# Attention that stores undivided sums channel by channel, and a row projection that divides and reads them with a step of four

## The chip, the cores and the metric

The kernel runs on one core of a Trainium2 chip. A core has a matrix engine (TensorE, PE in the profile, with its weight loads listed apart as PEld), VectorE (DVE), ScalarE (ACT), GpSimd (POOL) and a queue processor (SyncE, SP). Transfers between the chip's memory (DRAM here) and the core's SBUF are moved by 16 DMA engines. The metric is the device time of one launch in microseconds, as the median of some runs; lower is better.

## What is computed

One transformer layer on x of shape (4, 2048, 256), all in float32. Cut to what matters here:

```
y    = softmax(causal(q k^T / 4)) v          16 heads of 16 channels, per batch of 2048 tokens
x1   = x + concat_heads(y) @ Wc              the row projection: 8192 tokens x 256 channels
n    = layernorm(x1);  logits = n @ Wr + br  the router, 8 experts, top 2
out  = x1 + sum over 2 experts of gate * (relu(n @ W1 + b1) @ W2 + b2)
```

The change is in how y is divided by its softmax sums and how it reaches `y @ Wc`.

## The kernel before

The kernel is written as four stages, one behind another with a barrier between each: `project` (layernorm and the products that make q, k and v), `attend`, `mix` (the row projection, second layernorm and router) and `experts`. Each engine runs a list of instructions in its order and waits on semaphores.

**attend** goes through 16 windows w. A window is one batch and a group of GH = 4 heads over all 2048 tokens. It has CH = 4 chunks of TB = 512 query tokens, and chunk c has 4(c+1) steps of 128 key tokens, so a window has NSTEP = 40 steps. Three kinds of work are interleaved on TensorE. A `max` piece (L1004) makes scores of 128 queries of two heads in a bank pair `ps_m`, and VectorE takes their maxima (L888, and L892 on the diagonal); this runs a window ahead. A `scores` group (L963) makes transposed scores with the maximum already taken off, and ScalarE takes their exponential (L865). A `sum` step (L984) multiplies four heads' exponentials by v with a column of ones, into `ps_o`: per head, 16 rows of values and a 17th that is the softmax sum, 32 partitions apart, with the 512 queries along the row. After a chunk's last step ScalarE copies `ps_o` to `out_sb` (L871).

A fourth kind, `turn_out`, stands 64 times in the list (16 windows, 4 chunks). TensorE turns the chunk's `out_sb` with four transposes into a `ps_m` slot (L1015), VectorE takes the reciprocal of the sums (L926) and multiplies (L931) into `y_sb`, and SP stores 128 KB to `y_dram`, in which a row is a token (L757).

What sets the order of the four kinds is `attention_plan`, run when the kernel is built: it keeps estimated clocks of the engines and picks the kind that can start first, shifted by `HOLD`. All engines walk the same list, `PLAN`. The `ps_m` slots are two, used in turn (`ring`), and TensorE waits for a slot's last reader before it writes it.

On SP's queue, behind the last step of window w, stand 13 transfers that load window w+3 (L716 and L724, 256 KB each but the last), then the store of the last chunk, then the maxima of the next window (L733 and L739), and so on, as `PLAN` has them.

**mix** goes through NB = 16 tiles of 512 tokens in NB+2 iterations. TensorE turns the loaded rows of y (`turn_y`, L1452), ScalarE copies them to `yt` (L1206), TensorE multiplies by Wc (`mix_heads`, L1467), VectorE adds x to make `x1` (L1328) and takes the layernorm. ScalarE applies it, TensorE turns the result, forms the logits (L1479), and two iterations later VectorE picks the two experts and makes `slots`, whereon GpSimd issues 8 indirect transfers for the tile that scatter entries to `list_dram` (L1189, 128 in all). SP loads y and x four tiles ahead (`load_y` L1136, `load_x` L1139), stores x1 (L1161) and fetches a part of the expert weights per tile (L1143). A tile's token t = 4q + j is partition q, row j.

**experts** begins with loads of `list_dram`, so it waits for all 128 scatters, and walks 142 tiles of 128 rows.

## Time and profile before

| | us |
|---|---|
| median of 3 runs | 2670.48 |
| lowest and highest | 2664.89, 2671.22 |
| the profiled execution, its own time | 2660.48 |
| its span, first to last instruction | 2658.8 |
| granted TensorE clock, mean of the span | 0.948 |

Busy time in the span: TensorE 2356.7 us (89%), VectorE 2044.3 (77%), ScalarE 1581.8 (59%), GpSimd 824.5 (31%). The stages stand in the trace roughly so: `project` to about 260 us, `attend` to 1930, `mix` to 2131, `experts` to the end. A busy time is an average over stages with different limits, so the stages have to be read apart.

### The profile page before, as it was taken

The page shows a single profiled execution, that of the slowest core. Times are in us where ns is not written, and L with a number is a line of the kernel's source. Part 1 is how long each engine was busy: PE and PEld are TensorE (multiplying, and loading weights), DVE is VectorE, ACT ScalarE, POOL GpSimd, SP SyncE. Part 2 cuts the span into 40 slices and gives each one's busy share as a digit, 9 for nine tenths or more (in the row PEclk, how much of TensorE's full clock was granted, in tenths as well). Part 3 has the DMA queues.
Part 4 walks back from the last instruction along what each step waited for, and adds up shares of the span by engine and source line. Part 5 has one row for each costly group of instructions (what it writes and reads, how often), then busy time and mean ns, then how long its engine had stood idle before and what let it go on. Part 6 is the DMA issues. An engine that isn't in the chain of part 4 may idle for free. (4 is left out here: it accounts for less than half of the span.)

```text
span 2658.8 us, 48214 instructions
## 1 busy us (share of the span) xinstructions
PE 2356.7 (89%) x15842; PEld 1342.6 (50%) x15842; DVE 2044.3 (77%) x5000; ACT 1581.8 (59%) x2716; POOL 824.5 (31%) x1132
## 2 busy tenths in 40 slices
PE   6786699999999999999999999998879379999998
PEld 6675233333343333333333333333256168998897
DVE  3785988988989899888889988993068557777776
ACT  3663177776777777766777777777745234444443
POOL 1444021121122112112112112112137755566554
PEclk7998599999999999999999999999989689999999
DMA  3777824135045045044144144101099323333332
GB/s 136 260 267 222 118 45 76 41 60 119 30 63 89 28 65 89 28 64 76 42 63 74 45 65 73 45 8 31 21 296 281 115 89 114 107 105 109 111 110 71
DMA packets 147718, 256.02 MB, mean 96 GB/s; under 512 B 72968, under 2 KB 92042, under 8 KB 139157
## 3 DMA queue, kind: packets, MB, share of 16 engines
q1 hardware_dynamic: 114544, 164.96, 28.0%
q0 software_dynamic: 29904, 80.65, 9.2%
q10 hardware_dynamic: 3028, 7.33, 1.7%
q8 instruction: 135, 2.21, 0.4%
q14 instruction: 107, 0.87, 0.1%
HBM read 147.65 MB, written 107.76 MB: 96 GB/s over the span
## 5 line engine op out<-in xcount | busy, mean ns | idle before, releaser
L865 ACT ACTIVATE prob<-ps_s 128x512 f32<-128x512 f32 (+5 forms) x1620 | 1078.5, 714 | 464.8 <-PE ps_s L963 462.2
L888 DVE TENSOR_REDUCE maxes<-ps_m 128x2 f32<-128x1024 f32 x768 | 914.1, 1222 | 112.6 <-PE ps_m L1004 109.3
L963 PE MATMUL ps_s<-q_st,k_st 50*128 50x512 f32 (+3 forms) x2560 | 605.4, 409 | 78.9 <-ACT prob L865 56.9
L1004 PE MATMUL ps_m<-k_st,q_st 48*128 48x512 f32 (+3 forms) x2560 | 605.1, 444 | 75.2 <-DVE maxes L888 39.6
L814 POOL TENSOR_SCALAR_AFFINE_SELECT prob<-prob 128x256 f32<-128x256 f32 x512 | 203.2, 406 | 1341.8 <-ACT prob L865 1211.9
L984 PE MATMUL ps_o<-prob,v_sb 128*17 128x512 f32 (+3 forms) x5120 | 606.7, 547 | 1.4 <-ACT prob L865 0.7
L1004 PEld LDWEIGHTS ps_m<-k_st,q_st 48*128 48x128 f32 x2560 | 273.6, 192 | 531.2 <-DVE maxes L888 261.3
L892 DVE CUSTOM_DVE_ANT_0 junk<-ps_m,causal 128x128 f32<-128x128 f32 (+3 forms) x1024 | 453.0, 484 | 47.6 <-PE ps_m L1004 45.9
L963 PEld LDWEIGHTS ps_s<-q_st,k_st 50*128 50x128 f32 x2560 | 316.6, 188 | 299.9 <-ACT prob L865 222.0
L1741 ACT ACTIVATE h_hi<-ps_turned 128x512 fp32r<-128x512 f32 x142 | 84.9, 598 | 213.9 <-PE ps_turned L1856 212.4
L94 PE MATMUL ps_out<-experts_hi,h_lo 128*128 (+1 forms) x568 | 171.6, 302 | 0.1
L984 PEld LDWEIGHTS ps_o<-prob,v_sb 128*17 128x17 f32 x5120 | 86.5, 95 | 168.5 <-issue 138.4
L96 PE MATMUL ps_out<-experts_hi,h_hi 128*128 (+1 forms) x568 | 160.4, 282 | 0.0
L95 PE MATMUL ps_out<-experts_lo,h_hi 128*128 (+1 forms) x568 | 160.1, 282 | 0.0
L1189 POOL DMA_INDIRECT list_dram<-entry,slots x128 | 123.9, 968 | 76.2 <-issue 39.6
L1770 DVE TENSOR_TENSOR h<-ps_hidden,b_sb 128x512 f32<-128x512 f32 x142 | 98.3, 692 | 43.9 <-PE ps_hidden L96 43.4
L1784 DVE TENSOR_TENSOR y<-ps_out,b_sb 128x256 f32<-128x256 f32 x142 | 60.3, 425 | 87.0 <-PE ps_out L96 87.0
L94 PE MATMUL ps_hidden<-experts_hi,x_lo 128*128 (+1 forms) x284 | 125.5, 442 | 0.3 <-issue 0.2
L96 PE MATMUL ps_hidden<-experts_hi,x_hi 128*128 (+1 forms) x284 | 112.6, 396 | 0.0
L95 PE MATMUL ps_hidden<-experts_lo,x_hi 128*128 (+1 forms) x284 | 112.4, 396 | 0.0
L1731 ACT ACTIVATE xn<-rows,lists 128x256 f32<-128x256 f32 x142 | 84.0, 591 | 47.1 <-DMA rows<-rows_dram,lists 46.2
L95 PEld LDWEIGHTS ps_out<-experts_lo,h_hi 128*128 128x128 f32 x568 | 107.6, 189 | 0.1
(187 smaller groups left out, 3065.8 us busy)
## 6 DMA issues: line engine op xcount, KB each, us to landing
parts_dram<-parts SPq DMA_DIRECT2D x64, 512.0 KB, 3.8
q_st<-parts_dram SPq DMA_DIRECT2D x84, 256.0 KB, 8.9
k_st<-parts_dram SPq DMA_DIRECT2D x84, 256.0 KB, 18.2
v_dram<-v_out SPq DMA_DIRECT2D x16, 544.0 KB, 5.5
xin<-in_L_attn_x SPq DMA_DIRECT2D x16, 512.0 KB, 6.0
ffn_raw<-in_L_ffn_W POOLq DMA_DIRECT2D x32, 256.0 KB, 5.2
y_dram<-y_sb SPq DMA_DIRECT2D x64, 128.0 KB, 2.0
split_hi<-ffn_hi POOLq DMA_DIRECT2D x16, 512.0 KB, 3.2
```

The source lines that it names most:

```text
L94: nc.tensor.matmul(out, s_lo, m_hi, start=first, stop=False, skip_group_check=True)
L95: nc.tensor.matmul(out, s_hi, m_lo, start=False, stop=False, skip_group_check=True)
L96: return nc.tensor.matmul(out, s_hi, m_hi, start=False, stop=last, skip_group_check=True)
L814: nc.gpsimd.affine_select(out=tile, in_=tile, compare_op=ALU.is_ge, fill=0.0, base=0, pattern=[[0, 2], [1, P]], channel_multiplier=-1).the ...
L865: last_exp = nc.scalar.activation(prob[:, at:at + n, lo:TB], bank[:, 0:n, lo:TB], ACT.Exp, scale=DH ** -0.5)
L888: return nc.vector.tensor_reduce(maxes[:, 2 * pair:2 * pair + 2, qt, kc], bank[:, :, :], AX.X, ALU.max)
L892: last = nc.vector.tensor_tensor_reduce(junk[:, slot, i, 0:w], bank[:, i, 0:w], causal[:, TB - w:TB], 1.0, NEG, ALU.add, ALU.max, maxes[:, ...
L963: mm = nc.tensor.matmul(ps_s[k % 2][:, i, lo:TB], k_st[half(h % 2, ROWS), w % BUFS, h // 2, kt * P:(kt + 1) * P], q_st[half(h % 2, ROWS), ...
L984: mm = nc.tensor.matmul(ps_o[32 * h:32 * h + VW, lo:TB], v_sb[:, w % BUFS, kt, h, :], prob[:, (s % PROBS) * GH + h, lo:TB], start=STEP_FIR ...
L1004: mm = nc.tensor.matmul(ps_m[slot][:, i, 0:wide], q_st[half(i, STACK), w % BUFS, pair, qt * P:(qt + 1) * P], k_st[half(i, STACK), w % BUFS ...
L1189: pool.indirect_dma_start(list_dram[:, :], bass.IndirectOffsetOnAxis(ap=slots[:, j, i:i + 1], axis=0), entry[:, j, i, :], None).then_inc(s ...
L1770: nc.vector.tensor_tensor(out=h[:, s % 2, :], in0=ps_h[s % 2][:, :], in1=b1_sb[:, bass.ds(e, 1), :].rearrange("p a n -> p (a n)"), op=ALU. ...
```

## The change

**In attend**, `turn_out` is gone: the four transposes, the reciprocal and the product of a chunk, with `y_sb` and `rec`. SP stores `out_sb` as it is, 256 KB a chunk, to a `y_dram` whose row is a channel (32 rows for each of the 16 heads: 16 of values, the sum, the rest unused) and whose columns are the 8192 tokens. Sums are divided apart: at step 3 of window w, SP loads the 2048 x 4 sums of window w-1 as 128 rows of 64; at step 12 VectorE takes their reciprocal in place; at step 20 SP stores them to `inverse_dram`, one row per head. ScalarE's copy of chunks 0 and 1 waits for the stores of the window before. `PLAN` is made anew without `turn_out`, so pieces shift against each other. A helper transfer of numbers (L834) is replaced by an iota on GpSimd.

**In mix**, `turn_y` and ScalarE's copy to `yt` are gone. A tile of y is loaded as two transfers of 8 heads x 16 channels x 512 tokens, and the inverses as two more of the same size, each head's row repeated for its 16 channels. VectorE multiplies the two in place (`scale_heads`, 128 x 1024). The product with Wc takes its stationary operand from the scaled tile directly; since token t = 4q + j must come to partition q, 128 columns are read with a step of four elements. The last window's sums are fetched, inverted and stored at the start of mix.

```diff
-                elif e[0] == "turn_out":
-                    ...
-                    sp.dma_start(to.rearrange("(j p) n -> p j n", p=P),
-                                 y_sb[:, c % 2, :, :, :].rearrange("p j h d -> p j (h d)")
-                                 ).then_inc(y_stored[c % 2], 16)
+                elif e[0] == "sum":
+                    w, c, _ = STEP_LIST[e[1]]
+                    step = e[1] % NSTEP
+                    if w and step == INVERSE_LOAD:
+                        for u in range(2):
+                            sp.wait_ge(y_stored[u], 32 * w)
+                        ...
+                        load_sums(sp, w - 1, inverse[:, (w - 1) % 2, :], sums_in)
+                    elif w and step == INVERSE_STORE:
+                        sp.wait_ge(inverse_made, w)
+                        store_inverse(...)
+                    if STEP_LAST[e[1]]:
+                        sp.wait_ge(out_copied, w * CH + c + 1)
+                        sp.dma_start(y_dram[w % HG * P:(w % HG + 1) * P, ...], out_sb[:, c, :])
+                    if e[1] + 1 == (w + 1) * NSTEP and w + BUFS < NG:
+                        sp.wait_ge(summed, e[1] + 1)
+                        load(sp, w + BUFS)
...
+                elif e[0] == "sum" and e[1] >= NSTEP and e[1] % NSTEP == INVERSE_MADE:
+                    w = e[1] // NSTEP - 1
+                    dve.wait_ge(sums_in, 16 * (w + 1))
+                    nc.vector.reciprocal(inverse[:, w % 2, :], inverse[:, w % 2, :]).then_inc(inverse_made, 1)
...
+                for a in range(CC):
+                    sp.dma_start(y_in[:, n % YB, a, :],
+                                 y_v[a * HP:(a + 1) * HP, 0:DH, tokens]).then_inc(y_loaded[n % YB], 16)
...
+                    sp.dma_start(inverse_in[:, n % 2, a, :],
+                                 inverse_dram[a * HP:(a + 1) * HP, tokens].unsqueeze(1).broadcast_to([HP, DH, TB])
+                                 ).then_inc(y_loaded[n % YB], 16)
...
+                if n + 2 < NB:
+                    sp.wait_ge(y_scaled, n + 1)
+                    load_inverse(n + 2)
...
+            def scale_heads(n):
+                dve.wait_ge(y_loaded[n % YB], 32 * CC * (n // YB + 1))
+                tt(out=y_in[:, n % YB, :, :], in0=y_in[:, n % YB, :, :], in1=inverse_in[:, n % 2, :, :],
+                   op=ALU.mult).then_inc(y_scaled, 1)
...
-                                                yt[:, a, j * P:(j + 1) * P], wc_sb[:, a, :],
+                                                y_in[:, n % YB, a, :].rearrange("p (q j) -> p j q", j=TILES)[:, j, :], wc_sb[:, a, :],
```

TensorE in attend, from the last step of chunk 0 to the first of chunk 1 of window 6 (`ps_m` maxima, `ps_s` scores, `ps_o` sums; a row is a line, an output, its inputs and its shape). Before:

```order
L984 MATMUL ps_o<-prob,v_sb 17x128 x4
L1004 MATMUL ps_m<-k_st,q_st 128x256 x2
L963 MATMUL ps_s<-q_st,k_st 128x384 x2
L1004 MATMUL ps_m<-k_st,q_st 128x256 x2
L963 MATMUL ps_s<-q_st,k_st 128x384
L1015 MATMUL ps_m<-ident,out_sb 128x128 x4
L984 MATMUL ps_o<-prob,v_sb 17x512 x4
```

and in the changed kernel, whose lines have other numbers (L988 is the sum, L1008 the maxima, L967 the scores):

```order
L988 MATMUL ps_o<-prob,v_sb 17x128 x4
L967 MATMUL ps_s<-q_st,k_st 128x384 x2
L1008 MATMUL ps_m<-k_st,q_st 128x512 x2
L967 MATMUL ps_s<-q_st,k_st 128x384
L1008 MATMUL ps_m<-k_st,q_st 128x256 x2
L988 MATMUL ps_o<-prob,v_sb 17x512 x4
```

The four transposes are gone, and the maxima stand in other places beside the same scores.

SP in attend, around the load of a window (q, k and v to `q_st`, `k_st`, `v_sb`). Before:

```order
L716 DMA q_st<-parts_dram 16x2x2048 x6
L716 DMA k_st<-parts_dram 16x2x2048 x6
L724 DMA v_sb<-v_dram 128x1088
L757 DMA y_dram<-y_sb 128x4x64
L733 DMA minus_dram<-minus_rows 16x2x128
L739 DMA q_st<-minus_dram 2x2x512 x2
```

and in the changed kernel:

```order
L769 DMA y_dram<-out_sb 128x512
L708 DMA q_st<-parts_dram 16x2x2048 x6
L708 DMA k_st<-parts_dram 16x2x2048 x6
L716 DMA v_sb<-v_dram 128x1088
L721 DMA inverse<-y_dram 128x1x64
L769 DMA y_dram<-out_sb 128x512
L734 DMA minus_dram<-minus_rows 16x2x128
L740 DMA q_st<-minus_dram 2x2x512 x2
```

The last chunk's store has moved ahead of the 13 loads, and the sums are fetched directly behind them.

SP in mix, one tile. Before (x rows, expert weights, then y of the tile four ahead; `b_sb` and `x_own` are the buffers of y and x):

```order
L1161 DMA rows_dram<-x 128x1024
L1139 DMA x_own<-in_L_attn_x 128x1024
L1143 DMA experts_lo<-split_lo 128x2048
L1136 DMA b_sb<-y_dram 128x1024
```

and in the changed kernel:

```order
L1171 DMA rows_dram<-x 128x1024
L1144 DMA x_own<-in_L_attn_x 128x1024
L1148 DMA experts_lo<-split_lo 128x2048
L1131 DMA b_sb<-y_dram 128x1x512 x2
L1139 DMA inverse_in<-inverse_dram 128x1x512 x2
```

The y load is two transfers in place of one, of the same bytes, and two of inverses, again the same bytes, stand behind it.

## Rows read from the trace of the kernel before

**Rows 1.** Busy time by stretch: us, then busy (instructions) per engine, PEclk, DMA share, GB/s.

```profile
430.00:1834.00 1404.00, 1302.82 (x9224) 541.45 (x9224) 1235.51 (x2689) 1016.37 (x1618) 262.38 (x532) 0.98 0.33 59
1834.00:1930.00 96.00, 78.03 (x501) 26.01 (x497) 3.41 (x10) 72.06 (x118) 17.12 (x36) 0.98 0.06 19
1970.00:2060.00 90.00, 82.30 (x552) 59.31 (x551) 74.52 (x482) 50.35 (x102) 68.35 (x72) 1.00 1.01 274
```

**Rows 2.** Groups by line: busy us, mean ns of one, idle before it and its releaser.

```profile
L1015 PE MATMUL ps_m<-ident,out_sb 128*128 128x128 f32 x256 | 42.2, 288 | 9.3 <-DVE maxes L888 4.9 <-DVE maxes L892 1.5 <-ACT out_sb L871 1.4
L931 DVE TENSOR_TENSOR y_sb<-ps_m,rec 128x256 f32<-128x256 f32 x64 | 27.2, 424 | 4.7 <-DMA y_dram<-y_sb 2.6
L926 DVE RECIPROCAL rec<-ps_m 128x16 f32<-128x16 f32 x64 | 16.2, 254 | 112.0 <-PE ps_m L1015 111.1
L888 DVE TENSOR_REDUCE maxes<-ps_m 128x2 f32<-128x1024 f32 x768 | 914.1, 1222 | 112.6 <-PE ps_m L1004 109.3
L386 DVE TENSOR_TENSOR turned<-turned,swapped 128x512 f32<-128x512 f32 x32 | 21.5, 711 | 0.0
```

**Rows 3.** The tile y_sb: who waited for it (us, times).

```profile
  PE ps_m L1004: 3.3, 4
```

**Rows 4.** Timeline, the end of attend: start, us, engine, line.

```profile
1925.79 0.58 ACT L871 COPY out_sb<-ps_o 128x512 f32<-128x512 f32 x1 [1.17 <-PE ps_o L984]
...
1927.92 0.36 SPq L757 DMA_DIRECT2D y_dram<-y_sb  x1
1930.35 0.36 ACTq L1199 DMA_DIRECT2D numbers<-in_tile_numbers  x1
```

**Rows 5.** Timeline of SP at a window's end, the load of the next.

```profile
1030.54 2.66 SPq L716 DMA_DIRECT2D q_st<-parts_dram  x6
...
1036.04 0.42 SPq L724 DMA_DIRECT2D v_sb<-v_dram  x1
1036.50 0.44 SPq L757 DMA_DIRECT2D y_dram<-y_sb  x1
```

**Rows 6.** Tile y_sb in 1030 to 1045 us: landing of that store.

```profile
DMA to landing us min/median/max: 22.8/22.8/22.8
```

**Rows 7.** Timeline of ACT: copy of that window's last chunk, next window's chunk 1.

```profile
1030.61 0.59 ACT L871 COPY out_sb<-ps_o 128x512 f32<-128x512 f32 x1
...
1058.74 0.59 ACT L871 COPY out_sb<-ps_o 128x512 f32<-128x512 f32 x1
```

**Rows 8.** Stretches as in rows 1: mix before scatters; head loads; two small transfers.

```profile
1950.00:1960.00 10.00, 8.45 (x47) 5.91 (x46) 7.53 (x32) 6.34 (x13) 0.00 (x0) 1.00 1.00 385
...
1038.00:1054.00 16.00, 15.07 (x123) 6.97 (x125) 15.48 (x43) 11.66 (x21) 3.15 (x8) 1.00 1.03 126
...
512.60:513.60 1.00, 0.38 (x5) 0.02 (x2) 1.00 (x2) 1.00 (x2) 0.00 (x0) 1.00 0.09 37
```

**Rows 9.** DMA issues in 509 to 514 us: KB each.

```profile
q_st<-minus_dram SPq DMA_DIRECT2D x2, 24.0 KB
```

**Rows 10.** DMA issues in 1970 to 2060 us: KB each, median us to landing.

```profile
rows_dram<-x SPq DMA_DIRECT2D x10, 512.0 KB, 12.5
experts_hi<-split_hi SPq DMA_DIRECT2D x5, 1024.0 KB
...
b_sb<-y_dram SPq DMA_DIRECT2D x7, 512.0 KB, 17.5
```

**Rows 11.** Timeline of mix: the same step of two tiles on DVE.

```profile
2009.74 1.29 DVE L1328 TENSOR_TENSOR x<-ps_x,x_own 128x512 f32<-128x512 f32 x2
...
2018.52 1.29 DVE L1328 TENSOR_TENSOR x<-ps_x,x_own 128x512 f32<-128x512 f32 x2
```

**Rows 12.** Line 1467, the product with Wc: duration ns min/median/max.

```profile
L1467 PEld LDWEIGHTS ps_x<-wc_sb,yt x256: 186/190/337, 1938.5 to 2068.3; 128*128 128x128 f32 x128
L1467 PE MATMUL ps_x<-wc_sb,yt x256: 379/379/792, 1938.5 to 2068.5; 128*128 128x256 f32 x128
```

**Rows 13.** Timeline of POOL: first scatters of mix, last scatter.

```profile
1966.69 1.05 POOL L1189 DMA_INDIRECT list_dram<-entry,slots  x1 [34.80 <-DVE slots L1437]
...
1984.61 0.96 POOL L1189 DMA_INDIRECT list_dram<-entry,slots  x1 [0.30 <-issue]
...
2130.96 0.97 POOL L1189 DMA_INDIRECT list_dram<-entry,slots  x1 [0.31 <-issue]
```

More of the change, by code:

```diff
@@ L473 @@
 BUFS = 3
-HOLD = {"max": -171, "scores": -140, "sum": 0, "turn_out": -266}
+HOLD = {"max": -171, "scores": -140, "sum": 0}
+HEAD_ROWS = 32
+INVERSE_LOAD, INVERSE_MADE, INVERSE_STORE = 3, 12, 20
 STEP_LIST = [(w, c, kt) for w in range(NG) for c in range(CH)
@@ L593, in attention_plan @@
             k += 1
-        elif kind == "sum":
+        else:
             plan.append(("sum", s))
@@ L603, in attention_plan, with attend @@
                 loaded[s // NSTEP + BUFS - 1] = end + 45000
-        else:
-            plan.append(("turn_out", outs.pop(0)[0]))
-            tile_free[:], issued = [start + 430, start + 430], start + 430
-            vector = max(start + 630, vector - 85) + 700
-            taken.append(vector)
     return plan
-def attend(nc, parts_dram, v_dram, w1, w2, minus_dram, y_dram, split_dram, tile_numbers, rows_dram, pairs_dram,
+def attend(nc, inverse_done, parts_dram, v_dram, w1, w2, minus_dram, y_dram, inverse_dram, split_dram, rows_dram, pairs_dram,
            list_dram):
@@ L1029, with mix @@
 XB = 4
-def mix(nc, x, y_dram, wc, wr, br, split_dram, tile_numbers, w_sb, b1, b2, biases, biases_in, block, slots_made, scattered, numbers, run, entry, slots, rows_dram,
+def mix(nc, inverse_done, x, y_dram, inverse_dram, wc, wr, br, split_dram, tile_numbers, w_sb, b1, b2, biases, biases_in, block, slots_made, scattered, numbers, run, entry, slots, rows_dram,
         pairs_dram, list_dram):
@@ new lines, in transformer_block @@
+    with ExitStack() as whole:
+        inverse_done = [whole.enter_context(nc.semaphore(name))
+                        for name in ("sums_in", "inverse_made", "inverse_stored0", "inverse_stored1")]
+        attend(nc, inverse_done, parts_dram, v_dram, w["L0_ffn_W1"], w["L0_ffn_W2"], minus_dram, y_dram, inverse_dram, split_dram,
+               rows_dram, pairs_dram, list_dram)
+        with ExitStack() as ctx:
+            w_sb = [ctx.enter_context(nc.sbuf_tensor(f"experts_{half}", [P, CHUNKS, WCH], F32R)) for half in ("hi", "lo")]
+            biases = [ctx.enter_context(nc.sbuf_tensor(name, [P, E, width], F32))
+                      for name, width in (("b1_sb", F), ("b2_sb", C))]
+            biases_in = ctx.enter_context(nc.semaphore("biases_in"))
+            slots_made = ctx.enter_context(nc.semaphore("slots_made"))
+            scattered = ctx.enter_context(nc.semaphore("scattered"))
+            block = ctx.enter_context(nc.Block())
+            numbers = ctx.enter_context(nc.sbuf_tensor("numbers", [P, SLOT_TILES], F32))
+            run = ctx.enter_context(nc.sbuf_tensor("run", [P, 2, TOP, E], F32))
+            entry = ctx.enter_context(nc.sbuf_tensor("entry", [P, NT, TOP, WORDS], I32))
+            slots = ctx.enter_context(nc.sbuf_tensor("slots", [P, NT, TOP], I32))
+            mix(nc, inverse_done, w["L0_attn_x"], y_dram, inverse_dram, w["L0_attn_Wc"], w["L0_ffn_Wr"], w["L0_ffn_br"], split_dram,
+                w["tile_numbers"], w_sb, w["L0_ffn_b1"], w["L0_ffn_b2"], biases, biases_in, block, slots_made, scattered, numbers, run, entry, slots, rows_dram, pairs_dram, list_dram)
+            experts(nc, block, slots_made, scattered, w_sb, numbers, run[:, NB % 2, :, :], entry, slots, biases, biases_in, rows_dram, pairs_dram,
+                    list_dram, out)
```

155 lines of the change are left out of this document (62 added, 93 removed).

## The prediction

> **What bounds the kernel now.** I read the stretches of the busy-time table first, then the groups by line, then the timeline where an edit lies. In `attend` (first line of [rows 1]) PE is busy for 1302.8 of 1404 us and DVE for 1235.5; a `turn_out` is work for both, and each waits for the other on the two `ps_m` slots. Taking work from both shortens the stage, and neither can hide the other's saving. In the last window (second line of [rows 1]) ACT has 72 of 96 us and DVE 3: little is won there. In `mix` (third line of [rows 1]) the DMA engines are full (share 1.01, 274 GB/s), and one thing stands behind them: GpSimd's scatters. The first starts at 1966.69, the last at 2130.96 [rows 13]; 127 steps in 164.3 us are 1.29 us each, so a tile's eight take 10.2 to 10.3, nearly without a pause. `experts` waits for all of them. So `mix` ends when POOL ends, and POOL is fed by DVE, which is fed by loads. A DVE tile takes 8.78 us [rows 11], the DMA's pace, and runs ahead of POOL. Whatever makes a tile's loads longer than 10.2 us moves the end.
>
> **Attend, what goes.** PE: 64 groups of transposes are 42.2 us busy, 9.3 idle ahead of them [rows 2], and 3.3 in which the next maxima waited for `y_sb` [rows 3]: 54.8. Windows 0 to 14 hold 60 of the 64: 51. DVE: 16.2 (reciprocals) + 27.2 (products) + 2.6 (wait for a store) = 46.0 [rows 2], by 60/64: 43. Both are full, so the gain lies between; DVE's maxima wait for PE for 109.3 us in all [rows 2], which are PE's rhythm, not free time. I take 45, bounds 43 to 51; only if the freed slots are not filled (the remaining pieces follow other dependencies) does it fall to half. The end: the last copy starts at 1925.79 and ends at 1926.37, transposes, product and a store at 1927.92 follow, and `mix` begins at 1930.35 [rows 4]. The store now follows the copy: about -2.
>
> **Attend, what comes.** One reciprocal a window, 128x64, 15 times. The 128x16 one takes 254 ns (L926 in [rows 2]), and 64 elements at the maxima's 1222 / 1024 ns (L888) are 76: 0.2 to 0.33 us each, +3. Its wait is the new thing: DVE stands at step 12 until the sums are in, and all maxima queue behind it. The sums' transfer stands directly behind the 13 loads, 3.7 MB, which began at 1030.54 [rows 5] and run at 126 GB/s with the queue full (second line of [rows 8]). The store that stood there, issued at 1036.50, landed 22.8 us later [rows 5, 6], at 1059.3, which is 28.7 us after the window's copy at 1030.61; chunk 1 of the next window was copied at 1058.74 [rows 7], 28.1 us in, and step 12 is the end of that chunk's steps. So the sums come at about 29 to 32 and DVE asks at about 31 to 33. I take +3 for 13 windows; bounds 0 and, if each stands 2 to 4 us, 26 to 52. Ahead of the loads SP now also waits for the last chunk's copy, 0.6 us [rows 7], inside that. ACT's new wait, for a store from a window before, is for transfers that stand ahead of the loads and have a chunk's time to land: 0. The inverses' store at step 20 has 80 us to land: 0. Dropping `first_numbers` is 0 (one load, once).
> Sum of attend: -45 - 2 + 3 + 3 = **-41**.
>
> **Mix, engines.** PE loses a tile's transposes, ACT a copy: neither sets the pace (POOL and the DMA do): 0. DVE gains a product of 128x1024 from SBUF. The 128x512 one on SBUF takes 0.71 (L386 in [rows 2]), twice that 1.42; a reduction of 1024 takes 1.22. DVE's share of a stretch is 74.5 of 90 [rows 1], 7.3 us a tile; 8.7 fits below 10.2: 0, while it would cost 16 x 1.4 = 22 if DVE were the bound. The operand read with a step of four: weight loads of 190 ns between products of 379 [rows 12], 16 a tile; nothing shows what a step costs. Bounds: nothing, or loads three times as long, 16 x 0.38 = 6.1 us a tile. PE is busy for 82.3 of 90 us [rows 1], 8.0 of a tile; 8.0 + 6.1 = 14.1, less the transposes that it loses, which is still about the DMA's tile below. So 0, but under rival 1 it would cost from 2 us a tile on.
> The Trainium skill, page "SBUF — State Buffer", section "Door 1: The DMA port swizzle", has SBUF lines of 16 bytes, and each access that goes to a new line pays; a step of four float32 is a new line for each element. No row of before shows such a read. By that the weight loads would be longer; the sum would not change as long as they stay covered.
>
> **Mix, transfers.** The two loads of y are the same bytes, and 0.5 MB of inverses is added to a tile of y 0.5, x 0.5, rows 0.5, experts 1.0 MB [rows 10]. What decides is how many engines carry the new forms. Two transfers whose outer count is 2 (24 KB in all) [rows 9] were under way in 512.6 to 513.6 and the share there was 0.09 at 37 GB/s (third line of [rows 8]): 0.09 x 16 = 1.5, so about two engines out of 16. The new loads have an outer count of 8 (heads), against 128 before. I take 8 of the 16 engines, the same ones each time.
> The Trainium skill, page "DMA: Bandwidth & Descriptors", section "Why a DMA increments its semaphore by 16 and not by 1", says just this: the number of engines is the largest up to 16 that divides the slowest dimension of both sides, here 8 and 128, the lowest-numbered ones. The row of the two agrees.
> Speed of an engine: 385 GB/s at share 1.00 before the scatters (first line of [rows 8]), 24.1 each. Under scatters it is 274 [rows 1]: 24.6 MB in 90 us would take 64 at 385; the 26 lost fall on 90 / 1.27 = 71 scatters, 0.38 us each. On a low engine a tile is now y 65.5 KB + inverses 65.5 + a sixteenth of 2.0 MB, 131: 262 KB / 24.1 = 10.9 us, + 8 x 0.38 = **13.9 us**, over POOL's 10.2.
> The last tile's inverses have ahead of them on such an engine 3.90 MB (y and inverses of 16 tiles 2.10, x 0.52, rows and experts of 13 tiles 1.28): 162 us, + 11 tiles of scatters 33, + 4 to start: from 1930 to 2129. In that iteration `slots` of tile 11 follows, at 2131.5, and from there POOL has tiles 11 to 15, 40 scatters at 1.27, 51 us: 2182 against 2132. **+50.** Bounds: if all 16 engines carried them, a tile would be 3.0 MB / 385 = 7.8 + 3.0 = 10.8 us, +0.6 on POOL's 10.2 for a dozen tiles: +8; if the pieces of 2 KB went at the head loads' 126 / 16 = 7.9 GB/s an engine, each tile of y would take 8.3 rather than 2.7 us, 5.6 x 16 = 90 more: +140. I take +50, since mix's own loads are nearer in kind.
>
> **Sum.** 2660.5 - 41 + 50 = 2669.5 on the profiled execution's time. The median of three is 10.0 above that one: **2679**, +0.3%.
>
> **The rivals.**
> (1) Other side, faster: the 16 engines share the loads, or scatters don't slow an engine that is already the late one. Then mix is POOL's, the row stage costs +8 and not +50, the rest is -33: 2638. It decides by whether a tile on the loads' engines stays under 10.2 us. For it: without the 3.0 a tile has 10.9; against it: the row of the two-part transfers.
> (2) The small pieces are slow: +90 on the forecast: 2769. For it: 126 GB/s under the head loads; against it: those are other strides, and y is read in long rows.
> (3) The sums come late and DVE stands 2 to 4 us in each of 13 windows, 26 to 52 in place of 3: 2702 to 2728. For it: the landing at 28.7 is within 3 us of when it is asked for, and one window's rhythm is not another's. Against: DVE is itself late in a window.
> (4) Attend gains only half, -20 in place of -41: 2700. The plan's estimates are not of the chip, and pieces moved; PE may turn out to wait for ACT. ACT has 72% of its time [rows 1], so it is not next by much, but its exponentials follow the scores.
> (5) That the change doesn't do what it says: the order of instructions shows the transposes gone and the loads in place, so no chance of its own.
>
> **How the numbers follow.** Forecast 0.45, with its own range from 2663 to 2695 (attend by 43 to 51, the scatters' part of 3.0 a tile by a third either way). Rival 1 0.25, rival 2 0.07, rival 3 0.10, rival 4 0.13. The range: 2632 (rival 1 with an attend of -47) to 2712 (rival 4, half of rival 3); rival 2 and the rest of 3 are outside. About 8 us, 0.3%, is what a measurement of this kernel can tell from no change. Below 2662: rival 1 and a little of the forecast, 0.26. Within 2662 to 2678: some 0.20 of the forecast and 0.02 of others, 0.22. Above: 0.52.
>
> **What would show it.** Attend: its windows some 2.6 us shorter (41 / 16), no wait of DVE on `y_dram` data before the reciprocal above 1 us (rival 3 if 2 to 4). Mix: DVE's tile period near 13.9 with its wait on a load of `inverse_in`, DMA share about 0.8 (half of the engines at 13.9 of 13.9 us, the others at 5.4 + 3.0), POOL idle between tiles for DVE's `slots`, last scatter near 2141. Rival 1: period 10.2 to 10.8, share near 1.0, POOL unbroken. Rival 2: period near 20. Weight loads of L1467's successor longer than 190 ns but PE waited for by nobody. It is wrong above all if the new loads use more engines than 8, and if DVE's wait for sums is long.

## The result, and the profile after

The changed kernel takes 2740.44 us (median of four, 2727.90 to 2756.70), the kernel before 2670.85 beside it: a ratio of 1.0266 with a 95% interval of 1.0209 to 1.0324. Ratios, here and below, are taken over fast executions alone and can differ a little from the quotient of the two medians. The forecast was 2679 in a range up to 2712; the time lies 28 us above the range, and the change is slower by 70 us.

The stages, from the last copy of `out_sb` and the last scatter in each trace:

| | before | after |
|---|---|---|
| start to the last copy of attend | 1925.8 | 1935.9 |
| from there to the last scatter (row stage) | 205.2 | 273.2 |
| `experts` | 527.7 | 527.5 |

So 10 us are lost up to the end of attend, where 41 were to be won, and 68 in the row stage, where 50 were to be lost. (The 10 us are this pair's: over all traces, below, attend is as long as before.) Stretches of the changed kernel (us, then busy and instructions per engine, PEclk, DMA share, GB/s), to be held against [rows 1]:

```profile
430.00:1834.00 1404.00, 1297.87 (x8960) 525.67 (x8958) 1200.68 (x2585) 1013.05 (x1610) 260.97 (x527) 0.95 0.33 65
1936.00:2209.00 273.00, 148.12 (x738) 104.82 (x738) 149.90 (x838) 63.51 (x129) 126.04 (x133) 0.76 0.68 200
2000.00:2100.00 100.00, 64.56 (x330) 45.71 (x328) 58.10 (x329) 28.55 (x59) 53.49 (x55) 0.83 0.78 225
```

In attend TensorE is as busy as before, with the transposes gone, but its clock is 0.95 of full and not 0.98: it needs longer for the same products. In the row stage every engine idles (TensorE is busy for 148 of 273 us, GpSimd for 126), and the DMA share is 0.78 with 225 GB/s, where it was 1.01 with 274. It would look so if some of the 16 engines were full and others not; the experiments test it.

Who waits in the row stage (engine and line, what for, us, times, longest):

```profile
POOL list_dram L1199 <- DVE slots L1460: 106.2, 14, 63.9
DVE rank L1261 <- DMA numbers<-in_tile_numbers: 100.9, 1, 100.9
DVE b_sb L1332 <- DMA inverse_in<-inverse_dram: 85.1, 14, 10.1
```

GpSimd, without a pause in the kernel before [rows 13], waits 106 us for `slots`, 63.9 of them ahead of its first scatter (34.8 before). VectorE, which makes them, waits 85 us for the inverses, in 14 of 16 tiles (the second row is its idle time through the last window of attend). Three scatters with their waits, and the last two loads that gate:

```profile
2004.57 1.07 POOL L1199 DMA_INDIRECT list_dram<-entry,slots  x1 [63.94 <-DVE slots L1460]
...
2120.85 0.97 POOL L1199 DMA_INDIRECT list_dram<-entry,slots  x1 [5.81 <-DVE slots L1460]
...
2134.81 0.97 POOL L1199 DMA_INDIRECT list_dram<-entry,slots  x1 [4.08 <-DVE slots L1460]
```

```profile
2117.99 1.23 DVE L1332 TENSOR_TENSOR b_sb<-b_sb,inverse_in 128x1024 f32<-128x1024 f32 x1 [7.20 <-DMA inverse_in<-inverse_dram]
2119.90 0.17 DVE L1460 CAST slots<-slot 128x8 int32<-128x8 f32 x1
2131.95 1.22 DVE L1332 TENSOR_TENSOR b_sb<-b_sb,inverse_in 128x1024 f32<-128x1024 f32 x1 [5.46 <-DMA inverse_in<-inverse_dram]
2133.86 0.17 DVE L1460 CAST slots<-slot 128x8 int32<-128x8 f32 x1
```

The first scatter comes 68.7 us after the last copy (40.9 before), since the slots of tile 0 stand on VectorE behind the scaling of tile 4, and so behind five tiles of loads. From tile 0 to tile 9 a tile takes 14.5 us ((2134.81 - 2004.57) / 9) and each has a wait. From tile 9 on GpSimd is the bound, as it was all along before. So of the 68 us some 28 are the later first scatter and some 38 the nine tiles, 14.5 us each against 10.2.

The new instructions themselves:

```profile
L1332 DVE TENSOR_TENSOR b_sb<-b_sb,inverse_in 128x1024 f32<-128x1024 f32 x16 | 19.6, 1224 | 85.1 <-DMA inverse_in<-inverse_dram 85.1
L937 DVE RECIPROCAL inverse<-inverse 128x64 f32<-128x64 f32 x15 | 8.2, 548 | 51.3 <-DMA inverse<-y_dram 51.3
```

```profile
L1486 PEld LDWEIGHTS ps_x<-wc_sb,b_sb x256: 307/329/337, 1959.5 to 2158.4; 128*128 128x128 f32 x128
L1486 PE MATMUL ps_x<-wc_sb,b_sb x256: 379/420/812, 1959.5 to 2158.6; 128*128 128x256 f32 x128
```

Against [rows 12] a weight load with a step of four takes 329 ns in place of 190.

### The profile page after: what moved, and what is told of

It is laid out like the page before. It is cut to its first block and busy times, and to the rows that moved or that the text cites. A ratio compares the mean times of both kernels' runs of the same rounds, so it can differ in the third digit from the quotient of the medians.

```text
span 2736.6 us, 47289 instructions
## 1 busy us (share of the span) xinstructions
PE 2368.8 (87%) x15458; PEld 1335.0 (49%) x15458; DVE 2027.9 (74%) x4904; ACT 1566.0 (57%) x2684; POOL 828.1 (30%) x1132
## 5 line engine op out<-in xcount | busy, mean ns | idle before, releaser
L967 PE MATMUL ps_s<-q_st,k_st 50*128 50x512 f32 (+3 forms) x2560 | 619.9, 415 | 79.0 <-ACT prob L874 52.6
L1008 PE MATMUL ps_m<-k_st,q_st 48*128 48x512 f32 (+3 forms) x2560 | 607.1, 450 | 90.1 <-DVE maxes L900 49.4
L988 PE MATMUL ps_o<-prob,v_sb 128*17 128x512 f32 (+3 forms) x5120 | 628.7, 564 | 1.8 <-ACT prob L874 0.7
L1008 PEld LDWEIGHTS ps_m<-k_st,q_st 48*128 48x128 f32 x2560 | 273.5, 194 | 587.3 <-DVE maxes L900 300.7
L967 PEld LDWEIGHTS ps_s<-q_st,k_st 50*128 50x128 f32 x2560 | 324.4, 193 | 306.3 <-ACT prob L874 226.3
L988 PEld LDWEIGHTS ps_o<-prob,v_sb 128*17 128x17 f32 x5120 | 86.8, 96 | 176.1 <-issue 141.9
L1486 PE MATMUL ps_x<-wc_sb,b_sb 128*128 128x256 f32 x256 | 87.0, 512 | 70.2 <-DVE x L1349 52.0
L1486 PEld LDWEIGHTS ps_x<-wc_sb,b_sb 128*128 128x128 f32 x256 | 72.6, 329 | 81.6 <-issue 41.2
```

Source lines behind the costliest of these rows:

```text
L967: mm = nc.tensor.matmul(ps_s[k % 2][:, i, lo:TB], k_st[half(h % 2, ROWS), w % BUFS, h // 2, kt * P:(kt + 1) * P], q_st[half(h % 2, ROWS), ...
L988: mm = nc.tensor.matmul(ps_o[32 * h:32 * h + VW, lo:TB], v_sb[:, w % BUFS, kt, h, :], prob[:, (s % PROBS) * GH + h, lo:TB], start=STEP_FIR ...
L1008: mm = nc.tensor.matmul(ps_m[slot][:, i, 0:wide], q_st[half(i, STACK), w % BUFS, pair, qt * P:(qt + 1) * P], k_st[half(i, STACK), w % BUFS ...
L1486: last = nc.tensor.matmul(ps_x[j // 2][:, (j % 2) * C:(j % 2 + 1) * C], y_in[:, n % YB, a, :].rearrange("p (q j) -> p j q", j=TILES)[:, j, ...
```

## The experiments

They ran on five chips, and the chips are of two kinds. On two, as on the first, the kernel before takes 2672 to 2676 us; on three, 2730 to 2743. So each run is read against the runs of the kernel before on its own chip, and stage times are compared within a kind.

### Two kinds of chip

The kernel before was profiled three times more. In `before_b`:

> The kernel before, profiled on the chip of the runs beside it. On the chip of the last four runs it took 2730 us where it takes 2670 on the first, and the changed kernel 2769 where it takes 2740. If that chip is only slower in all stages alike, the row stage and the experts are here as long as there (205 and 528 us) times one factor. If signals arrive late in the row stage and the experts, as the traces of the four runs show (TensorE done, the next engine starting 2 to 6 us after it), the extra stands in those two stages alone and attend is 1499 us again, with 40 to 80 us at half clock.

It took 2680.11 us, with a row stage of 205.5 and `experts` of 527.7, on a chip of the first kind; its attend had 123 us at half clock, where 40 to 80 were expected. `before_c`:

> The kernel before once more, for its clock: its two traces show 59 and 125 us at half clock in attend with a length of 1499 and 1522 us from the fourth chunk's copy to the last, the changed attend 118 to 183 us in six traces. If the clock is the same lottery in both, this one lies anywhere between 59 and 183; if the changed order loses more, it is under 130. The length less 0.37 times the half-clock time is 1475 to 1478 in either case.

2735.01 us, row stage 246.7, `experts` 553.0, on a chip of the second. And `before_d`, of the second kind too:

> The kernel before, a fourth trace: half-clock time in attend under 130 us (so far 59, 125, 75), its length less 0.37 times that 1475 to 1480. Over 130 us would say that the changed attend's 116 to 181 are the same lottery.

2732.16 us, 245.6 and 548.5. On the second kind attend is no longer (1506 and 1509 us from the fourth copy to the last, 1499 and 1522 on the first), and the row stage and `experts` lose 41 and 21 to 25 us: so it is not one factor on all stages. What the traces show in these two stages, on all three chips of the second kind and on none of the first, are late signals. Waits of the row stage in `before_c`, and the tile that shows one:

```profile
ACT xt L1206 <- remote: 39.5, 9, 6.8
```

```profile
2061.17 1.04 PE L1452 MATMUL ps_turn<-ident,xn 128*128 128x128 f32 x8
...
2065.98 1.08 ACT L1206 COPY xt<-ps_turn 128x512 f32<-128x512 f32 x2 [5.59 <-remote]
```

TensorE ends its transposes at 2062.21, ScalarE starts on them 3.8 us later, and nothing of the kernel lies between ("remote": no releaser in the profile). On such a chip the kernel before itself no longer keeps GpSimd fed, so the change costs less there. What delays the signals stays open, and so does whether they are all of the 60 us.

### The changed kernel again

> The changed kernel beside it on the same chip: 2728 to 2770 us. Attend (first chunk copies to the last) 5 to 20 us longer than in the kernel before, with 130 to 185 us at half clock against some 60; row stage 68 to 80 us longer.

On the chip of `before_b`: 2728.25 us, ratio 1.0196 (1.0159 to 1.0233), row stage 272.4, 67 us over `before_b`. Attend is 10 us shorter than in `before_b` (1511 against 1522) and not 5 to 20 longer, because `before_b` itself lost much clock.

> The changed kernel beside the others on this chip: ratio to the kernel before 1.015 to 1.03, 116 to 181 us at half clock in attend.

On another of the first kind: 2735.58 us, ratio 1.0251 (1.0194 to 1.0308), row stage 269.2, 126 us at half clock: as expected.

> The changed kernel as it is, beside the others on one chip. In its first trace the row stage was 273 us (last copy of attend at 1935.9, last scatter at 2209.1) and attend had 163 us at half clock, against 59 in the kernel before. Both theories: 2728 to 2757 us. If the clock's loss belongs to the changed order of TensorE's work, half-clock time in attend is again over 110 us; if it was chance, it lies anywhere between 40 and 170.

On one of the second kind: 2769.20 us against 2729.56, ratio 1.0169 (1.0110 to 1.0228), row stage 286.9. That is 12 us over the expected time, which was worked out for a chip of the first kind; the half-clock time, 130 us, is over 110 as expected for an effect of the changed order.

### Row stage: the eight engines

The loads with an outer count of 16:

```diff
-                                 y_v[a * HP:(a + 1) * HP, 0:DH, tokens]).then_inc(...)
+                                 y_v[a * HP:(a + 1) * HP, 0:DH, tokens].rearrange("h d n -> d h n")).then_inc(...)
...
-                                 inverse_dram[a * HP:(a + 1) * HP, tokens].unsqueeze(1).broadcast_to([HP, DH, TB])
+                                 inverse_dram[a * HP:(a + 1) * HP, tokens].unsqueeze(0).broadcast_to([DH, HP, TB])
```

> The loads of y and of the inverses, and Wc, take channels in the order (channel of the head, head), so that the outer count of each load is 16 and no longer 8; nothing else is changed. If eight engines carrying the new loads set the pace of the row stage: a tile falls from 14 to 10.8 us or less, DMA share rises from 0.77 to near 1, and the time falls by 35 to 50 us. If the stage is paced by the longer weight loads (329 ns with the step of four) and its late start: less than 10 us.

2755.02 us, ratio 1.0100 (1.0062 to 1.0138) beside 1.0169 of the changed kernel on the same chip: 14 us by the medians. Row stage 259.7 against 286.9, less by 27. DMA share:

```profile
2000.00:2100.00 100.00, 64.72 (x322) 43.69 (x322) 60.40 (x333) 28.21 (x57) 60.54 (x59) 0.85 0.95 235
```

0.95 with 235 GB/s, where `after_again` has 0.75 with 224 in this stretch on the same chip: with nothing else changed than the order of channels, the same bytes keep more of the engines busy. Each busy engine moves less (15.5 GB/s against 18.7), so the share alone does not measure the gain. The gain is 14 to 27 us and not 35 to 50, and 19 of the 27 are the earlier first scatter (52.4 us after the last copy against 71.3). On this chip a tile can hardly get shorter: it still takes 13.5 us, with `slots` held up by late signals, as in `before_c` (13.4).

The inverses' loads left out:

```diff
+                if n >= 2:
+                    return
                 tokens = slice(n * TB, (n + 1) * TB)
                 for a in range(CC):
                     sp.dma_start(inverse_in[:, n % 2, a, :],
```

> The loads of the inverses are left out from the third tile on (the inverses of the first two tiles are used again, so y is divided by other tokens' sums); y is still loaded over an outer count of 8. A low engine's tile loses 65.5 KB of 262, 2.7 us by 24.1 GB/s: from 13.9 to 11.2 us. If the bytes on eight engines set the pace, the row stage falls by some 30 to 40 us. If the step of four or the late start does, by less than 10.

2687.64 us, ratio 1.0063 (1.0042 to 1.0085) beside 1.0196 on the same chip: 41 us by the medians. Row stage 222.5 against 272.4, less by 50, somewhat more than expected. 16 of the 50 are the earlier first scatter (53.8 us after the last copy against 69.7), 34 the shorter tiles: 10.5 us each up to tile 9. GpSimd hardly waits behind its first scatter (51.6 us in all, 49.1 of them ahead of it). So the bytes of the inverses are the pace, and the step of four, which is still in it, is not; that it matters over how many engines bytes lie is what `spread` shows. One rival is left: the inverses are asked for two tiles ahead and y four. In `after` those of tile 13 were asked for at 2112.73 and scaled at 2131.95, 19 us later; no run asked for them earlier, so how much of VectorE's wait is the short lead is not known.

Both the outer count of 16 and weights without a step:

```diff
-                tt(out=y_in[:, n % YB, :, :], in0=y_in[:, n % YB, :, :], in1=inverse_in[:, n % 2, :, :],
-                   op=ALU.mult).then_inc(y_scaled, 1)
+                tt(out=yt[:, n % 2, :, :].rearrange("p a (j q) -> p a j q", j=TILES),
+                   in0=y_in[:, n % YB, :, :].rearrange("p a (q j) -> p a j q", j=TILES),
+                   in1=inverse_in[:, n % 2, :, :].rearrange("p a (q j) -> p a j q", j=TILES),
+                   op=ALU.mult).then_inc(y_scaled, 1)
```

> Loads of y and inverses with an outer count of 16, as in the run spread, and the scaled y written by VectorE in the order that TensorE reads, so that the weight loads have no step. If the eight engines are what costs, most of the gain is that of spread (20 to 30 us of the changed kernel's row stage of 273) and the weights add under 5. If TensorE's chain (weights of 329 ns against 190, 2.2 us a tile) is next in line once the loads are spread, both together give 40 to 60 us.

In the trace the row stage is 238.3, 34 less, with the DMA share at 1.01. The times say less: 2716.93 us, ratio 1.0175 (1.0151 to 1.0200) beside 1.0196, and the intervals overlap; the profiled execution, 2692.42, was the fastest of five. VectorE pays for the reordering:

```profile
L1337 DVE TENSOR_TENSOR yt<-b_sb,inverse_in 128x1024 f32<-128x1024 f32 x16 | 32.0, 1999 | 36.8 <-DMA inverse_in<-inverse_dram 36.7
```

1999 ns where the plain product takes 1224. How much of the 34 us is the weights' and how much the engines' is not known: `spread` and this run stand on chips of different kinds.

The late start:

```diff
+            sp.dma_start(wr_sb[:, :, :], wr.rearrange("(a p) n -> p a n", p=P)).then_inc(weights_in, 16)
+            sp.dma_start(br_sb[:, :], br.rearrange("(e a) -> e a", a=1)).then_inc(weights_in, 16)
             load_y(0)
```

> The router's weights and bias are asked for ahead of everything else in the row stage; in the changed kernel TensorE waited for them until 1959.5, behind the loads of two tiles, with its first tile scaled at 1951.6. If the late start is paid once and never made up: 8 to 20 us less. If the eight loaded engines set the end, they have the same bytes to carry and the start changes nothing: 0 to 4 us.

2775.41 us, ratio 1.0149 (1.0102 to 1.0196) beside 1.0169; row stage 288.7 against 286.9. TensorE's 8 us wait for the router's weights is real and costs nothing: the loads behind set the end.

### Row stage: no bytes added

```diff
+            def expand(n, a):
+                ...
+                nc.tensor.matmul(ps_i[:, :], spread[:, :], inverse_in[0:HP, n % 2, a, :], start=True, stop=True
+                                 ).then_inc(expanded, 1)
...
-                tt(out=y_in[:, n % YB, :, :], in0=y_in[:, n % YB, :, :], in1=inverse_in[:, n % 2, :, :],
+                tt(out=y_in[:, n % YB, a, :], in0=y_in[:, n % YB, a, :], in1=ps_i[:, :],
```

> The changed kernel with the inverses loaded once per head (8 rows of 2 x 512) and spread to the 16 channels by TensorE, one product with a matrix of zeros and ones per half tile into a bank of its own, from which VectorE multiplies (two of 128x512, the second behind the slots); channels in the order (channel, head), so that y is read over an outer count of 16; the router's weights are asked for first. A tile moves 2.5 MB as in the kernel before. If bytes and their eight engines are the whole of the row stage's loss: the row stage falls from 272 to 205 to 215 us (GpSimd's scatters without pause), the run 50 to 65 us under the changed kernel and 0 to 15 us around the kernel before. If the step of four or TensorE's chain sets the pace: still over 230.

2767.76 us, ratio 1.0108 (1.0050 to 1.0165), on a chip of the second kind; its row stage of 276.7 is 10 us shorter than the changed kernel's on another such chip, and 30 longer than that of the kernel before on its own. The expectation missed. A likely reason, not tested by itself, is that each tile has two more hand-overs between TensorE and VectorE, and on this kind of chip hand-overs are what is slow. On a chip of the first kind the same row stage took 234.9 (in `all_three`, below), and not 205 to 215. Of the 30 us over the kernel before, 21 are the later first scatter (61.9 us after the last copy against 40.9), and a tile takes 11.0 us up to tile 9 against 10.2; TensorE is now near its limit, 91 of 100 us busy.

```profile
2020.00:2120.00 100.00, 91.40 (x471) 58.23 (x470) 77.10 (x433) 36.24 (x74) 70.60 (x73) 0.97 0.91 237
```

### Attend: the transposes and the clock

The old order of attend is back, with its transposes, and nothing uses them:

```diff
+                elif e[0] == "turn_out":
+                    dve.wait_ge(piece_made, ring + 1)
+                    nc.vector.tensor_copy(seen[:, e[1], :], ps_m[slot][:, 0, 0:4]).then_inc(piece_taken, 1)
...
+                        for j in range(TILES):
+                            mm = nc.tensor.transpose(ps_m[slot][:, 0, j * P:(j + 1) * P],
+                                                     out_sb[:, e[1] % CH, j * P:(j + 1) * P], ident[:, :])
```

> The changed kernel with the old order of attend: the four transposes of each chunk stand where they stood, VectorE only reads 4 columns of them (64 times some 0.1 us), and nothing uses the result. TensorE has its 42 us of transposes again. If their absence is what lets the clock fall: half-clock time in attend falls from 163 us to under 80, and the stage is no longer than with them gone, the whole run -15 to +5 against the changed kernel. If the clock is chance or has another cause: half-clock time as in the changed kernel, and the run 20 to 45 us longer than it.

2792.81 us, ratio 1.0220 (1.0176 to 1.0264), 24 us over the changed kernel on its chip; half-clock time in attend 160 us. By this one trace the transposes' absence is not what lets the clock fall. With these traces a simple law came out. Half-clock time is the time at 1.2 GHz in the trace's record of the granted clock; the length is from the fourth copy of `out_sb` to the last:

| | length, us | half clock, us | length - 0.37 x half clock |
|---|---|---|---|
| before | 1499.2 | 58 | 1477.7 |
| before_b | 1521.7 | 123 | 1476.2 |
| before_c | 1506.1 | 75 | 1478.3 |
| before_d | 1509.4 | 85 | 1477.8 |
| turns_kept | 1538.2 | 160 | 1478.8 |
| after | 1514.3 | 164 | 1453.7 |
| after_again | 1504.7 | 130 | 1456.7 |
| after_b | 1511.4 | 157 | 1453.3 |
| after_c | 1501.1 | 126 | 1454.3 |
| spread, early, no_inverse, spread_packed, expand (attend unchanged) | 1497.5 to 1523.7 | 116 to 181 | 1454.0 to 1456.8 |
| sums_later | 1494.6 | 119 | 1450.4 |
| expand_sums | 1517.1 | 178 | 1451.4 |
| maxima_later | 1523.1 | 208 | 1446.2 |
| all_three | 1529.8 | 228 | 1445.4 |
| tail_filled (55 products more) | 1522.5 | 171 | 1459.4 |
| expand_tail (55 products more) | 1559.0 | 276 | 1456.8 |

The factor is a line through the nine traces of the changed attend (0.365; the four of the kernel before give 0.342). Both kinds of chip lie on it. So, at equal clock (the last column), the changed attend is 23 us shorter, and with the old order and its transposes back and VectorE's part of `turn_out` all but gone (64 reads of 4 columns) it is as long as before. The 23 us are the transposes' and those of their place in the order; which of the two is not told apart. VectorE's 43 were worth at most the few us that the new wait for the sums costs in `turns_kept` too (4.4 us in one window). And in the mean the changed attend has 152 us at half clock in place of 85, which takes 0.37 x 67 = 25 us back: its mean length is 1510.7 us, and 1509.1 before. Most of the difference stands behind the last maxima: 37 to 96 us at half clock there in the nine traces (mean 67), 3 to 14 in the four of the kernel before (mean 6). In `after` this is the stretch, where the kernel before has a PEclk of 0.98 (second line of [rows 1]):

```profile
1834.00:1930.00 96.00, 81.22 (x456) 24.81 (x456) 0.56 (x1) 67.89 (x112) 17.34 (x36) 0.82 0.06 23
```

More work for TensorE where it waits most:

```diff
+                    if s >= FILL_FROM:
+                        ...
+                        nc.tensor.matmul(ps_m[0][:, 0, 0:256], q_st[half(0, STACK), w % BUFS, 0, 0:P],
+                                         k_st[half(0, STACK), w % BUFS, 0, 0:256], start=True, stop=True)
```

> The changed kernel with one product of 128x256, into a bank that nobody reads, ahead of each of the last 55 sum steps of attend, where no maxima are left and TensorE waits for ScalarE. In the changed kernel the clock falls 5 us after the last maxima and is at half for 50 to 95 us of the last 145. If TensorE's thin work there is why: the half-clock time behind the last maxima falls under 15 us and attend is 10 to 20 us shorter. If the clock falls for another reason: half-clock time as before and attend the same or 5 to 10 us longer.

2801.33 us, ratio 1.0236 (1.0176 to 1.0296); 171 us at half clock, of them 94 behind the last maxima, where under 15 were expected. The theory falls: the filled end lost as much clock as the unfilled ones. With `expand`:

> Both: if both theories hold, 60 to 80 us under the changed kernel and 5 to 25 us under the kernel before (2650 to 2665 on the chips where that takes 2671). If only the bytes theory holds, as the run expand.

2812.96 us, ratio 1.0234 (1.0170 to 1.0299); half clock 276 us in attend, 187 of them in one piece that runs through the filled end and on to 218 us:

```profile
1790.00:1980.00 190.00, 173.17 (x681) 54.00 (x681) 0.55 (x1) 98.49 (x150) 23.31 (x42) 0.51 0.06 20
```

TensorE never stands for more than 0.82 us in that stretch of attend, so no pause explains this loss. In the same part of the kernel before it was busy for 83 of 99 us at a clock of 0.98, and did more (533 products in 99 us against 681 in 190, since a product at half clock takes longer):

```profile
1826.00:1925.00 99.00, 83.49 (x533) 27.42 (x529) 2.73 (x8) 78.11 (x126) 17.50 (x36) 0.98 0.06 17
```

Then the order of the maxima:

```diff
-HOLD = {"max": -171, "scores": -140, "sum": 0}
+HOLD = {"max": -120, "scores": -140, "sum": 0}
```

> The changed kernel with another weight in the planner's choice (maxima at -120 in place of -171), by which the last maxima stand in window 15 (0.28 in) and not in window 14 (0.60 in). If the long end without maxima costs clock: half-clock time behind the last maxima, 50 to 95 us now, falls under 30, and attend is 8 to 20 us shorter. If the planner's old order was better in itself: the windows at full clock are longer than 97.1 us and attend is longer.

2748.03 us, ratio 1.0293 (1.0240 to 1.0347) beside 1.0251. At equal clock attend is 8 us shorter (1446.2). Behind the last maxima 30 us are at half clock, against 48 in `after_c` on the same chip and near the 30 expected; but ahead of them it is 178 against 79, spread over many windows, and attend is 22 us longer and not 8 to 20 shorter. In this trace a tighter order of the same work lost more clock than it won: a shorter end moved the loss and did not remove it.

### Attend: the sums' wait

```diff
-INVERSE_LOAD, INVERSE_MADE, INVERSE_STORE = 3, 12, 20
+INVERSE_LOAD, INVERSE_MADE, INVERSE_STORE = 3, 20, 28
```

> The changed kernel with the reciprocal of the sums at step 20 in place of 12 and their store at step 28. If the wait for the sums costs: VectorE's wait before the reciprocal is under 1.2 us in every window, the 14 to 34 us of half clock behind window 4's are gone, and the run is 5 to 15 us under the changed kernel. If the clock falls there anyway: no difference beyond 5 us.

What it removes is seen in `after_b`, in the sixth window (window 4 of the expectations, which count from the fourth copy), and so in eight of the nine traces of the changed attend (`after` has no wait there). SP and VectorE, then TensorE:

```profile
833.78 0.42 SPq L716 DMA_DIRECT2D v_sb<-v_dram  x1
834.24 0.43 SPq L734 DMA_DIRECT2D minus_dram<-minus_rows  x1
856.41 1.23 SPq L740 DMA_DIRECT2D q_st<-minus_dram  x2
857.75 0.57 SPq L721 DMA_DIRECT2D inverse<-y_dram  x1
```

```profile
860.30 0.55 DVE L937 RECIPROCAL inverse<-inverse 128x64 f32<-128x64 f32 x1 [4.20 <-DMA inverse<-y_dram]
...
861.27 0.80 PE L1008 MATMUL ps_m<-k_st,q_st 48*128 48x512 f32 x2 [4.43 <-DVE maxes L904]
```

In this window the maxima's store and reload stand between the 13 loads and the sums. SP waits for the store, which waits in the queue behind 3.7 MB until 856.41, and only then asks for the sums. VectorE stands 4.2 us, TensorE 4.4, and the clock falls behind it (PEclk is the number before the last two):

```profile
850.00:860.00 10.00, 6.75 (x48) 2.68 (x48) 5.90 (x11) 6.32 (x12) 1.98 (x5) 0.99 0.60 120
860.00:870.00 10.00, 8.70 (x48) 4.31 (x48) 6.82 (x17) 3.61 (x7) 1.17 (x3) 0.50 0.10 36
870.00:880.00 10.00, 9.70 (x39) 3.50 (x43) 6.28 (x11) 5.09 (x8) 0.00 (x0) 0.50 0.00 0
```

`sums_later` has no wait over 1.1 us there and the clock at 1.00:

```profile
860.00:870.00 10.00, 9.51 (x70) 3.87 (x66) 9.72 (x19) 7.75 (x11) 0.11 (x1) 1.00 0.14 53
```

The window is 97.1 us long, against 108.2 in `after_c` on the same chip and 110.8 in `after_b`. The run: 2730.37 us, ratio 1.0207 (1.0150 to 1.0264) beside 1.0251. The trace shows that the wait and the fall behind it are gone. The whole of attend gained less clock by it: 119 us at half against 126 in `after_c`. By the times it is 5 to 12 us, within the intervals.

### The edits together

`expand` with both edits of attend:

> The run expand with both edits of attend. If all three causes hold: row stage 205 to 220 us on a chip without the late signals, attend 1475 to 1495 us with under 80 us at half clock, and the run 10 to 30 us under the kernel before (2640 to 2662 where that takes 2671). If only the bytes hold: about as the kernel before.

2716.74 us, ratio 1.0121 (1.0060 to 1.0182) beside 1.0251: the row stage is 34 us shorter (234.9), attend 29 us longer (1530, where 1475 to 1495 was expected), since the shortest length at equal clock (1445.4) went with 228 us at half clock. `expand` with the later sums alone:

> The run expand with the reciprocal of the sums at step 20. Row stage 230 to 240 us as in all_three (on a chip without the late signals), attend 1490 to 1515 us with 110 to 180 us at half clock: ratio to the kernel before 1.002 to 1.012. If attend's time were set by the work at full clock alone, it would be 22 us under the kernel before's, and the ratio 0.995 to 1.002.

2757.03 us against 2734.20, ratio 1.0054 (1.0024 to 1.0084; the quotient of the medians is 1.0084), the smallest of all complete versions, on a chip of the second kind, where the changed kernel itself stood at 1.0169. Row stage 277.5 and attend 1517 us with 178 at half clock: the sums' wait is gone, and the clock was lost in other windows. None of the versions beats the kernel before.

## Why the prediction was wrong

Three terms failed: attend's -45, which is 23 us at equal clock; the granted clock, which the sum put at nothing and which takes 25 us back; and the row stage's +50, which is 68.

- **What bounds the row stage**: right. GpSimd waits for `slots`, these for the inverses.
- **Eight engines, 13.9 us a tile**: right in mechanism, a little small in size. Measured 14.5; `no_inverse` and `spread` bear out bytes and engines. By the bytes counted there, 262 KB, an engine carried 18.1 GB/s, scatters included, where the prediction's 13.9 us make 18.9; whether the 24.1 GB/s of [rows 8] or the scatters' share was off is open.
- **+50 for the row stage**: the sum was short by 18. It gave the start 4 us; but tile 0's slots wait for five tiles of loads, and the first scatter came 28 us later than before. The sum followed only the last tile's load and did not ask from which tile on GpSimd is the bound again. That was tile 9 at 2134.8, with seven tiles of scatters still to go, and not tile 11 at 2131.5 with five.
- **Step of four covered**: right (`no_inverse` has it and loses 50 us of the stage all the same), at 139 ns a load more.
- **Rival 1**: its price was too low as well. With the loads over all engines and no step the stage is still 33 us over the kernel before, not 8.
- **Attend, -45 between 43 and 51**: this step failed. At equal clock it is 23. Two errors: the 12.6 us of TensorE's idle time around `turn_out` were counted as saved, but TensorE idles more and not less without it. And VectorE at 88% was taken for a second bound: with its part of `turn_out` gone and the transposes kept, nothing was won. Rival 4, half of the gain, had this size. Two windows at full clock each, in `before` and in `after`:

```profile
1339.80:1537.10 197.30, 184.23 (x1327) 77.07 (x1328) 178.54 (x397) 144.87 (x232) 37.45 (x76) 1.00 0.35 61
```

```profile
1338.90:1532.90 194.00, 177.80 (x1296) 73.93 (x1298) 175.51 (x380) 144.48 (x231) 37.35 (x76) 1.00 0.36 68
```

  TensorE has 6.4 us less work and the pair is 3.3 shorter: half of it became idle time (13.1 and 16.2 us), ahead of scores that wait for ScalarE and of maxima that wait for VectorE.
- **The reciprocals**: 548 ns, not 200 to 330; on VectorE, which is not the bound, it did not matter.
- **The sums' wait, +3**: right in most windows (0 to 2 us each) and wrong in one. The order of instructions was read at one window and taken for all; in another the maxima's store stands ahead of the sums, and SP's wait for it had to be counted. Rival 3 named this wait, but for all 13 windows, and none of the steps priced what a stop does to the clock: 3.7 to 5.4 us of waiting, and 14 to 31 us of half clock behind it, at 0.37 us each.
- **The clock was not in the prediction at all.** It decides attend: 23 us won, 25 taken back in the mean. In the profiled pair -41 turned to +10 and +50 to +68, and the sum is the 78 us between these two executions.
- **A reading**: the 24.0 KB of [rows 9] are those of each transfer, 48 in all, and not of the two together. The share of 0.09, on which the count of engines rests, is not touched by it.

Why the changed attend spends more time at half clock is explained in part only. Behind the sums' wait 22 us follow (mean of eight traces), and with the reciprocal later they are gone from that window. But `after`, which has no wait there, had 164 us at half clock all the same, and the three runs without the wait had 119, 178 and 228. The greater part stands behind the last maxima, and its cause stays open. The transposes' absence and thin work at the end are ruled out as far as one trace each goes, and an earlier end of the maxima moved the loss. Four traces with TensorE's work pressed closer or filled (`tail_filled`, `maxima_later`, `all_three`, `expand_tail`) had 171 to 276 us; but `turns_kept`, no fuller than the kernel before, had 160, so this is no explanation either.

## What to carry to other kernels

Count a load's outer dimension, not only its bytes: a layout that made it 8 in place of 128 cost here as if half of the DMA engines had to carry these loads alone, and the share of the profile, 0.78, does not look like a full queue. When work is taken off an engine that waits on others, expect its busy time back at most; here it was about half (23 of 42 us), and its idle time did not go. Follow the first tile of a pipeline as well as the last: 28 of the row stage's 68 us were its late start. And read the granted clock of the stretch before and after: of two orders of the same work the one shorter at equal clock was here not the shorter.

## What the hardware showed that was not expected

- A reciprocal costs 548 ns for 64 columns and 254 for 16 (those from `ps_m`), 6.1 ns a column more, where a reduction takes 1.2 (1222 ns for 1024).
- A weight load from SBUF with a step of four float32 takes 329 ns against 190. The Trainium skill, page "SBUF — State Buffer", section "Door 1: The DMA port swizzle", has a price for each access to a new line of 16 bytes; the trace agrees in direction, with a factor of 1.7. VectorE with two operands read so takes 1999 ns against 1224.
- The Trainium skill, page "DMA: Bandwidth & Descriptors", section "Why a DMA increments its semaphore by 16 and not by 1", has the engines chosen by the slowest dimension; DMA shares of 0.78 with a count of 8 and 0.95 to 1.01 with one of 16, at the same bytes, agree.
- A microsecond at half clock costs attend 0.37 us (13 traces), and TensorE stayed at half clock for 218 us in one piece in `expand_tail` without a pause of over 0.82 us up to attend's end.
- Three of six chips run the same kernel some 60 us longer, with waits of 2 to 7 us in the row stage (up to 6.8 in `before_c`) that no instruction of the kernel explains; `experts` has such waits too.
